# First keys prepared in two halves with their inputs split alike, one block's values copied inside the first chunk, and score tiles taken in another order

## The reference

```python
q, k, v = qkv[:, :, 0], qkv[:, :, 1], qkv[:, :, 2]      # [B, 1024, 16, 8]
q, k = _rmsnorm(q, q_scale), _rmsnorm(k, k_scale)
q, k = _apply_rope(q, k)
logits = jnp.einsum('bqhd,bkhd->bhqk', q * HEAD_DIM ** (-0.5), k)
out = jnp.einsum('bhqk,bkhd->bqhd', jax.nn.softmax(logits, axis=-1), v)
x = _layernorm(x + out.reshape(B, N, C) @ w_proj + b_proj)
h = jax.nn.silu(_tlin(x, w1_w, w1_s)) * _tlin(x, w2_w, w2_s)
h = jax.nn.gelu(_tlin(h, h1_w, h1_s), approximate=False)
h = jax.nn.gelu(_tlin(h, h2_w, h2_s), approximate=False)
x = _layernorm(x + _tlin(h, w3_w, w3_s))
```

## Time and profile before

| what | us |
|---|---|
| median of 3 runs | 377.18 |
| lowest and highest | 376.13, 378.87 |
| the profiled execution, its own time | 374.42 |
| its span, first to last instruction | 372.8 |
| mean granted TensorE clock in it | 0.983 |

### The profile page before, as it was taken

One profiled execution on the slowest core, in us unless ns is written; L12 is line 12 of the kernel. 1 busy time (PEld: TensorE's weight loads), 2 busy tenths in 40 slices (PEclk: granted clock), 3 DMA queues, 4 the chain that ended last, 5 costly groups with the idle time before them and its releaser, 6 DMA issues.

```text
span 372.8 us, 6252 instructions
## 1 busy us (share of the span) xinstructions
PE 339.6 (91%) x2087; PEld 134.4 (36%) x2091; DVE 221.6 (59%) x465; ACT 304.8 (82%) x350; POOL 28.7 (8%) x41
## 2 busy tenths in 40 slices
PE   7889989998999989998999999989999899999980
PEld 2412223222332444442222544433223535335850
DVE  2997978874557624464466462645477163567754
ACT  2699989999999889789999897979998987863330
POOL 2032111102100000001100000011000000011001
PEclk9989999998999999999999999999999999999996
DMA  7829454326212110201110200202021100000001
GB/s 228 288 77 357 134 184 177 150 98 230 85 38 81 48 55 2 69 33 62 67 62 38 89 11 6 94 0 104 24 94 39 68 0 0 0 29 0 2 0 33
DMA packets 12295, 29.42 MB, mean 79 GB/s; under 512 B 1138, under 2 KB 4082, under 8 KB 12274
## 3 DMA queue, kind: packets, MB, share of 16 engines
q1 hardware_dynamic: 8368, 16.23, 12.9%
q0 software_dynamic: 3328, 12.06, 9.0%
q10 hardware_dynamic: 578, 0.85, 0.7%
HBM read 17.64 MB, written 9.44 MB: 73 GB/s over the span
## 4 chain that ended last, share of the span: by engine, by line
PE 65%; DVE 13%; ACT 7%; DMA 6%; issue 5%; POOL 1%; SPq 0%; POOLq 0%; DVEq 0%; ACTq 0%
PE ps L490 24%; PE ps L537 15%; PE ps L476 12%; ACT probs L825 6%; PE ps L527 4%; PE ps L645 4%; DMA va<-v_all 4%; DVE ffn L1042 2%; PE ps L445 2%; PE ps L607 1%; DMA xT<-in_x_t 1%; DMA k_scr<-parts 1%; DVE r L923 1%; PE ps L679 1%; PE ps L507 1%
## 5 line engine op out<-in xcount | busy, mean ns | idle before, releaser
L825 ACT ACTIVATE probs<-ps 128x1024 f32<-128x1024 f32 x256 | 242.9, 1035 | 26.4 <-PE ps L476 26.3
L490 PE MATMUL ps<-probs,va 128*9 128x512 f32 x896 | 113.5, 598 | 2.7 <-ACT probs L825 2.4
L476 PE MATMUL ps<-qa,ka 32*128 32x512 f32 x512 | 76.2, 500 | 9.9 <-ACT probs L825 7.5
L476 PEld LDWEIGHTS ps<-qa,ka 32*128 32x128 f32 x512 | 31.1, 183 | 108.1 <-ACT probs L825 61.6
L1042 DVE TENSOR_SCALAR ffn<-ps,col 128x512 f32<-128x512 f32 x36 | 27.0, 750 | 54.9 <-PE ps L537 50.8
L537 PE MATMUL ps<-g_hi,w_hi 128*128 128x512 f32 x108 | 45.4, 421 | 2.5 <-DVE ffn L1042 2.5
L537 PE MATMUL ps<-g_lo,w_hi 128*128 128x512 f32 x108 | 42.3, 392 | 0.0
L490 PEld LDWEIGHTS ps<-probs,va 128*9 128x9 f32 x896 | 15.8, 89 | 48.1 <-issue 27.7
L537 PEld LDWEIGHTS ps<-g_hi,w_hi 128*128 128x128 f32 x108 | 20.2, 187 | 15.3 <-DVE ffn L1042 4.3
L1017 DVE TENSOR_TENSOR g_lo<-ffn,g_hi 128x512 fp32r<-128x512 f32 x36 | 24.9, 692 | 1.2
L423 POOL TENSOR_TENSOR rs<-ve,mhalf 128x4 f32<-128x4 f32 x6 | 6.1, 1022 | 229.9 <-DVE ve L1005 229.9
(11 more groups left out here) (129 smaller groups left out, 320.7 us busy)
## 6 DMA issues: line engine op xcount, KB each, us to landing
ka<-k_scr SPq DMA_DIRECT2D x14, 512.0 KB
k_scr<-parts POOLq DMA_DIRECT2D x8, 512.0 KB, 4.2
q_scr<-parts POOLq DMA_DIRECT2D x8, 512.0 KB, 5.0
qa<-q_scr SPq DMA_DIRECT2D x14, 256.0 KB
va<-v_all SPq DMA_DIRECT2D x14, 144.0 KB
ffn<-in_h POOLq DMA_DIRECT2D x1, 1024.0 KB, 6.8
h_raw<-in_h POOLq DMA_DIRECT2D x1, 1024.0 KB, 8.7
xT<-in_x_t SPq DMA_DIRECT2D x3, 256.0 KB, 6.6
```

The lines of the kernel that those rows point to most:

```text
L476: mm = pe.matmul(s_tile(u)[:, i, :], ka[rows, slot, kt * P:(kt + 1) * P], qa[rows, slot, :], start=True, stop=not shifted)
L490: mm = pe.matmul(ps[32 * h:32 * h + VW, O_BANK, :], v, probs[:, step % 4, h, :], start=(kt == 0), stop=(kt == KT - 1))
L825: nc.scalar.activation(probs[:, step % 4, 2 * pair:2 * pair + 2, :], s_tile(u), ACT.Exp).then_inc(exp_done, 1)
```

## The change

The change has four parts.

Input DMAs: the weights are stored in the order K, KS, Q, QS, V (`W_AT`) and come in two transfers of 128 KB; x of block 0 comes in two halves of 256 tokens (`HC` = 256 columns), the first on its own semaphore; cosines and sines are one DRAM tensor, loaded by one DMA for tokens 0 to 255, one for 256 to 511 and one for 512 to 1023, all from SyncE. `cols` goes over to ScalarE's queue.

First keys in two halves: projection, square, variance, Ln, Exp, rotation, sum and product of k0 are done for tokens 0 to 255 first, up to the strip rows; the same for tokens 256 to 511 stand behind the queries and the projections of k1. VectorE's order changes with it: the three strips of group 1 come right behind those of group 0, and the parts for the stores of k0 and q0 (`rows_parts(0, ...)`, `rows_parts(1, ...)`) behind them, ahead of those of k1.

Values of block 1: their projection is the new first task of the first chunk (slot 5) and ScalarE copies it behind pair 7. TensorE waits for the copy before the values of key tile 4. Before the first logits it waits for one copy and four logarithms.

Score tiles: they are taken in turn, but at pairs 43 and 54 the second oldest is taken instead of the oldest (`tiles_in_turn`), so that the last three pairs of a chunk have the tiles 0, 1, 2. A pair's logits wait for the exponential that last read its tile.

```diff
-MIX_FIRST = 18
+MIX_FIRST = 19
-TASKS = (("proj", 0), ("swap", 0), ("var", 0),
+W_AT = {K: 0, KS: P, Q: 2 * P, QS: 3 * P, V: 4 * P}
+TASKS = (("v", 1), ("proj", 0), ("swap", 0), ("var", 0),
...
-TASK_SLOTS = (10, 18, 22, 23, 26, 30, 31, 34, 38, 40, 42, 46, 48, 50, 54, 56, 59, 62)
+TASK_SLOTS = (5, 10, 18, 22, 23, 26, 30, 31, 34, 38, 40, 42, 46, 48, 50, 54, 56, 59, 62)
+V_PAIR = 7
+def tiles_in_turn(swaps):
+    order, found = [0, 1, 2], []
+    for u in range(2 * STEPS):
+        if u in swaps:
+            order[0], order[1] = order[1], order[0]
+        found.append(order.pop(0))
+        order.append(found[-1])
+    assert found[-3:] == [0, 1, 2]
+    return found
+TILE_SWAPS = (43, 54)
+TILE_OF = tiles_in_turn(TILE_SWAPS)
...
-            return ps[:, 2 * (u % 3):2 * (u % 3) + 2, :]
+            return ps[:, 2 * TILE_OF[u]:2 * TILE_OF[u] + 2, :]
...
-            sp.dma_start(wq[:, 0:4 * P], w_qkv[:, 0:4 * P]).then_inc(in_w, 16)
-            sp.dma_start(col[:, 0:NCOL], cols).then_inc(in_cols, 16)
-            sp.dma_start(sinT[:, 0:CH], sines[:, 0:CH]).then_inc(in_rope[0], 16)
+            sp.dma_start(wq[:, 0:2 * P], w_qkv[:, 0:2 * P]).then_inc(in_wk, 16)
+            load_tables(0, 0, HC)
+            sp.dma_start(wq[:, 2 * P:4 * P], w_qkv[:, 2 * P:4 * P]).then_inc(in_wq, 16)
+            load_tables(1, HC, CH)
             load_x(1)
             sp.dma_start(wq[:, 4 * P:5 * P], w_qkv[:, 4 * P:5 * P]).then_inc(in_wv, 16)
-            sp.dma_start(sinT[:, CH:SEQ], sines[:, CH:SEQ]).then_inc(in_rope[1], 16)
+            load_tables(2, CH, SEQ)
...
-                wait(pe, exp_done, 64 * c + (u - 2 if u >= 3 else (0, -2, -1)[u]) if u >= 3 or not isinstance(c, int) else 0)
+                before = max(v for v in range(-2 * STEPS, u) if TILE_OF[v % (2 * STEPS)] == TILE_OF[u])
+                if before >= 0 or not isinstance(c, int):
+                    pe.wait_ge(exp_done, 64 * c + before + 1)
...
                 if n == 0:
-                    pe.wait_ge(rot_done, 6)
+                    pe.wait_ge(rot_done, 8)
...
+                    if step == 1:
+                        pe.wait_ge(rot_done, 7)
                     logits(0, step, 0, shifted)
...
+                    if step == KT // 2 + 1:
+                        pe.wait_ge(v_evac, 2)
                     if step:
                         values(0, step - 1)
...
-            pe.wait_ge(in_w, 16)
-            pe.wait_ge(in_x[0], 16)
-            proj(K, ps[:, 0, :], 0).then_inc(qk_proj, 1)
-            proj(KS, ps[:, 1, :], 0).then_inc(qk_proj, 1)
+            pe.wait_ge(in_wk, 16)
+            pe.wait_ge(in_x_first, 16)
+            proj_half(K, ps[:, 0, 0:HC], 0).then_inc(qk_proj, 1)
+            proj_half(KS, ps[:, 1, 0:HC], 0).then_inc(qk_proj, 1)
             pe.wait_ge(in_means, 16)
             pe.wait_ge(sq_done, 1)
-            variance(ps[:, 4, :], sq_k).then_inc(var_ready, 1)
+            variance(ps[:, 5, 0:HC], sq_k[:, 0:HC]).then_inc(var_ready, 1)
+            pe.wait_ge(in_wq, 16)
+            pe.wait_ge(in_x[0], 16)
             proj(Q, ps[:, 2, :], 0).then_inc(qk_proj, 1)
             proj(QS, ps[:, 3, :], 0).then_inc(qk_proj, 1)
...
             proj(K, ps[:, MIX_BANK, :], 1).then_inc(qk_proj, 1)
+            proj_half(K, ps[:, 4, 0:HC], 1).then_inc(qk_proj, 1)
+            pe.wait_ge(ln_done, 1)
+            proj_half(KS, ps[:, 5, 0:HC], 1).then_inc(qk_proj, 1)
             proj(KS, ps[:, O_BANK, :], 1).then_inc(qk_proj, 1)
...
+            project_v(ps[:, 1, :], 0).then_inc(v_proj, 1)
             pe.wait_ge(ln_done, 2)
-            project_v(ps[:, 5, :], 0).then_inc(v_proj, 1)
             pe.wait_ge(sq_done, 3)
-            variance(ps[:, 4, :], sq_k1).then_inc(var_ready, 1)
-            pe.wait_ge(rot_done, 2)
-            project_v(ps[:, 0, :], 1).then_inc(v_proj, 1)
+            variance(ps[:, 0, :], sq_k1).then_inc(var_ready, 1)
+            pe.wait_ge(v_evac, 1)
+            pe.wait_ge(sq_done, 4)
+            variance(ps[:, 1, 0:HC], sq_k[:, HC:CH]).then_inc(var_ready, 1)
...
-            pe.wait_ge(v_evac, 2)
-            pe.wait_ge(ln_done, 3)
+            pe.wait_ge(ln_done, 4)
...
-            act.dma_start(xT[:, 0:CH], x_t[:, 0:CH]).then_inc(in_x[0], 16)
-            act.dma_start(cosT[:, 0:CH], cosines[:, 0:CH]).then_inc(in_rope[0], 16)
+            act.dma_start(xT[:, 0:HC], x_t[:, 0:HC]).then_inc(in_x_first, 16)
+            act.dma_start(col[:, 0:NCOL], cols).then_inc(in_cols, 16)
             act.dma_start(mean8[:], means).then_inc(in_means, 16)
+            act.dma_start(xT[:, HC:CH], x_t[:, HC:CH]).then_inc(in_x[0], 16)
...
+            def late_v(n):
+                act.wait_ge(mix_ready, n + 1)
+                copy_v(1, ps[:, MIX_BANK, :])
+                act.wait_ge(v_evac, 2)
+                act.nop().then_inc(mix_free, 1)
...
+                if u == V_PAIR:
+                    late_v(TASKS.index(("v", 1)))
...
+            turned_half(ps[:, 5, first], KS, 1, rot_k[:, second]).then_inc(rot_done, 1)
+            dve.wait_ge(sq_done, 4)
+            turned_half(ps[:, 4, first], K, 1, h_k[:, second]).then_inc(rot_done, 1)
+            rope_of(7, h_k[:, second], rot_k[:, second], rinv_k[:, second], 3)
+            direct_rows(h_k, HC, HC, 0, C_KLOW, ka[:, 0, second])
             turned_by(ps[:, MIX_BANK, :], K, 1, h_k1).then_inc(rot_done, 1)
-            rope_of(6, h_k1, rot_k1, rinv_k1, 3)
+            rope_of(8, h_k1, rot_k1, rinv_k1, 4)
             direct_rows(h_k1, 0, CH, 0, C_KLOW, ka[:, 0, CH:SEQ])
-            rows_parts(0, 0, 0, h_k)
-            rows_parts(1, 0, 1, h_q)
             direct_rows(h_k, 0, CH, 1, C_KLOW, ka[:, 1, 0:CH])
             direct_rows(h_q, 0, CH, 1, C_QLOW, qa[:, 1])
             direct_rows(h_k1, 0, CH, 1, C_KLOW, ka[:, 1, CH:SEQ])
+            rows_parts(0, 0, 0, h_k)
+            rows_parts(1, 0, 1, h_q)
             rows_parts(2, 1, 0, h_k1)
```

More of the change, by code:

```diff
@@ L98, in wait, with build @@
     eng.wait_ge(sem, count)
-def build(nc, x_t, x_n, w_qkv, cols, scale_rows, bias, w_proj, w1, w2, h1, h2, w3, cosines, sines, means, eye, out):
+def build(nc, x_t, x_n, w_qkv, cols, scale_rows, bias, w_proj, w1, w2, h1, h2, w3, tables, means, eye, out):
     ctx = ExitStack()
@@ L171, in build @@
         prep = probs[:].rearrange("p a h q -> p (a h q)")
-        sq_k, rinv_k, rot_k, sq_q, rinv_q, rot_q, sq_k1 = (prep[:, i * CH:(i + 1) * CH] for i in range(7))
+        sq_k, sq_q, rinv_q, rot_q, sq_k1 = (prep[:, i * CH:(i + 1) * CH] for i in range(5))
         held = [ffn[:, STAGE + i * CH:STAGE + (i + 1) * CH] for i in range(8)]
-        h_k, h_q, h_k1, rinv_k1, rot_k1 = held[0:5]
+        h_k, h_q, h_k1, rinv_k1, rot_k1, rinv_k, rot_k = held[0:7]
         late_sets = (held[5:8], held[2:5])
@@ L444, in proj, with proj_half @@
             def proj(i, bank, t):
-                return pe.matmul(bank, wq[:, i * P:(i + 1) * P], xT[:, t * CH:(t + 1) * CH], start=True, stop=True)
+                return pe.matmul(bank, wq[:, W_AT[i]:W_AT[i] + P], xT[:, t * CH:(t + 1) * CH], start=True, stop=True)
+            def proj_half(i, bank, hf):
+                return pe.matmul(bank, wq[:, W_AT[i]:W_AT[i] + P], xT[:, hf * HC:(hf + 1) * HC], start=True, stop=True)
             def project_v(bank, t):
                 for i in range(TILES):
-                    mm = pe.matmul(bank[:, i * P:(i + 1) * P], xT[:, t * CH + i * P:t * CH + (i + 1) * P], wq[:, V * P:(V + 1) * P],
+                    mm = pe.matmul(bank[:, i * P:(i + 1) * P], xT[:, t * CH + i * P:t * CH + (i + 1) * P], wq[:, W_AT[V]:W_AT[V] + P],
                                    start=True, stop=True)
@@ L776, in square, with logarithm, inverse_root, copy_v @@
                 nc.scalar.activation(dst, bank, ACT.Square).then_inc(sq_done, 1)
-            def inverse_root(n, bank, dst):
+            def logarithm(n, bank, dst):
                 act.wait_ge(var_ready, n)
                 nc.scalar.activation(dst, bank, ACT.Ln, bias=eps_c[:]).then_inc(ln_done, 1)
-                act.wait_ge(ln_done, n)
+            def inverse_root(ln, dst):
+                act.wait_ge(ln_done, ln)
                 nc.scalar.activation(dst, dst, ACT.Exp, scale=-0.5).then_inc(rinv_done, 1)
[L784 to L787, removed]
+            def copy_v(t, bank):
                 for i in range(TILES):
-                    ins = nc.scalar.copy(v_all[:, 0, :, (n - 1) * TILES + i, :, 0:HD],
+                    ins = nc.scalar.copy(v_all[:, 0, :, t * TILES + i, :, 0:HD],
                                          bank[:, i * P:(i + 1) * P].rearrange("p (g h d) -> p g h d", g=NG, h=HG))
@@ L793, in _ @@
             act.wait_ge(qk_proj, 1)
-            square(ps[:, 0, :], sq_k)
-            inverse_root(1, ps[:, 4, :], rinv_k)
+            square(ps[:, 0, 0:HC], sq_k[:, 0:HC])
+            logarithm(1, ps[:, 5, 0:HC], rinv_k[:, 0:HC])
+            inverse_root(1, rinv_k[:, 0:HC])
             act.wait_ge(qk_proj, 3)
             square(ps[:, 2, :], sq_q)
```

(32 more changed lines are left out.)

32 lines of the change are left out of this document (18 added, 14 removed).

## The result

The changed kernel takes 381.62 us (median of 20 runs, 380.40 to 384.25) where the kernel before took 377.01 (20 runs, 373.75 to 381.69) beside it. The ratio is 1.0159 with a 95% interval of 1.0134 to 1.0183: slower by 1.6%, beyond the 1% that I could tell from no change. The profiled execution took 381.76 us, span 380.0. Of the experiments, e10 and e12 have profiles of executions 4 and 6 us above their own medians; from those two only single stretches are read, no totals.

A forecast was written before the change was run, and what follows sets the result against it. It took step 16's wait for the load of group 2 as the first chunk's bound, TensorE behind it. 3.2 + 1.2 + 0.9 - 1.8 = +3.5 us on the median 377.18 gave 380.7 us; own range 379.0 to 382.5, all cases 376.0 to 384.3.

The forecast's parts named there:

- The sum of +3.5 us: Whole kernel: later load +3.2, slow clock +1.2, pair 43 +0.9, chunk boundaries -1.8 us.
- The key parts, moved behind the strips: Stores ahead of step 16: k0 issued at 30.2, k1 landing at 43.7, 5.5 us later issue, bounds 42.5 to 44.7.
- the old stream's thin place: DMA stream from k0's issue to k1's landing: a thinner place before k1's issue would go, saving 0.3 us.
- The opening: Kernel start: TensorE at 5.0, VectorE at 6.9, first logits near 16.2, first exponential near 17.1, 1.2 us earlier.
- The 0.6 us that I had left at pair 8: Opening: some 0.6 us gain left after the values' projection and copy, which only lengthens step 16's wait.
- The load: Load of group 2 for step 16: takes 13.2 us, lands at 57.0 in place of 53.8, +3.2 us.
- rival B: Step 16: load stretched to 15.1 us by weights and q1's store, two slow stretches; +6.7 us, 383.9; chance 0.15.
- The clock behind the wait: TensorE behind step 16's wait: throttled clock costs +1.2 us, bounds 0 and 3.4.
- Score tiles: Three chunk boundaries gain 0.6 us each, -1.8; pair 43 in the first chunk costs +0.9.
- Rival A: Step 16: load lands within 1 us of before and the clock holds; 376.3 us; chance 0.12.
- C: Step 16: the late load without a loss of clock; +2.3 us, 379.5; chance 0.17.
- D: Opening's gain of 0.6 to 1.2 us reaches the end, step 16 not bound by the load; 375.4; chance 0.06.

The follow-up runs named there:

- e10: The changed kernel with h2's load right behind h1 and the weights w1, w2, w3 issued behind q1's store; 373.65 us, ratio 0.9933.
- e12: e1 with the values' task of block 1 in slot 7 in place of 5, no dummy matmuls; 373.25 us, ratio 0.9916.
- e2: The kernel before with only the parts of k0 and q0 moved behind group 1's strips; 383.46 us, ratio 1.0206.
- e4: The changed kernel with 24 dummy matmuls before TensorE waits for the load of group 2; 381.54 us, ratio 1.0128.
- e1: The changed kernel with the parts of k0 and q0 put back ahead of group 1's strips; 373.87 us, ratio 0.9937.
- e3: The kernel before with the new order of score tiles alone; 377.24 us, ratio 1.0000.
- e6: e1 with three dummy matmuls ahead of the first logits; 373.31 us, ratio 0.9916.
- e7: e1 with the first chunk's tile swaps at pairs 45 and 53 in place of 43 and 54; 373.16 us, ratio 0.9922.
- e5: The changed kernel with h2's 1 MB load moved from between the stores to right behind h1; 379.97 us, ratio 1.0088.
- e9: e8 with the weight loads of w1, w2, w3 moved behind q1's store; 373.38 us, ratio 0.9941.
- e11: The kernel before with the weight loads of w1, w2, w3 moved behind q1's store; 375.56 us, ratio 0.9990.
- e8: e1 with h2's load behind h1, three opening dummy matmuls, first-chunk swaps at 45 and 53, values' task in slot 7; 371.36 us, ratio 0.9872.

## Why the prediction was right or wrong

The direction of the mechanism was right, the time of 380.7 us was 0.9 us short of the measured median, and the measured one lay in the range. That it came so near is in part luck. The sum of +3.5 us was read from the profiled execution of 374.42 us; from profile to profile the change cost 7.2 us, twice as much. I added the sum to the median of 377.18, which is 2.8 us above that execution, and the changed kernel has no such distance (381.76 profiled, 381.62 in the median). The two errors nearly cancel. The forecast's words "+0.9%" were too mild: I gave "within 1%" 0.55 and slower by more 0.40, and it was slower by 1.6%.

*The key parts, moved behind the strips: right in its chain, too small in its size.* The step gave 43.8 for SyncE's issue and +3.2 us at step 16; it was 46.41, and +6.7 by TensorE's start, beyond my bound of 6.1. The 3.5 us by which the wait ended later than forecast (60.5 in place of 57.0) are three terms. k0's issue at 30.66 in place of 30.2: 0.5. The stream from there to k1's landing: 15.6 us where I took the old 13.8 less 0.3, so 2.1. The load: 14.1 us where I took 13.2, so 0.9.

The stream's error is a step of its own: I assumed that the old stream's thin place came from the late issue of k1 and would go when k1 was issued early. It grew instead: 1.9 us at 246 GB/s before (31.1 to 33.0), 4.0 us at 246 GB/s in the changed kernel (from 36.6), with 347 and 323 on both sides. From the kernel before:

```profile
31.10:33.00 1.90, 1.48 (x16) 0.49 (x12) 1.80 (x5) 1.90 (x3) 0.01 (x1) 1.00 0.97 246
```

This repeats: from k0's issue to k1's landing the stream takes 15.6 to 15.8 us in the changed kernel, e2 and e4, where k1 is issued 3.5 us behind k0, and 13.8 or 13.9 us in the kernel before, e1, e3, e6, e7 and e12, where it is issued 8.3 us behind. Taking h2 out (e5) took 5.1 us off k1's landing, and the three stores alone ran at 326 GB/s, 3 MB in 9.3 us. That this slow place is h2's load between the stores fits both, but what slows it was not tried.

*The opening.* TensorE started at 4.46 where I took 5.0, and VectorE at 7.65 where I took 6.9. What it waited for was none of the things that I named: the row of scales, now last of five transfers on ScalarE's queue, landed at 6.87 and the flags from it took until 7.65. The first logits at 16.40 and the first exponential at 16.98 are within 0.2 us of my step. The 0.6 us that I had left at pair 8 were wrong in sign: it started at 28.42 where it had been 26.69, with 6.8 us of slow clock and the values' task in step 2 both in it. So TensorE was free for step 16 at 54.51 and not at 51.8, and its wait was 6.03 us long only because the load came so late. As I said, none of this reached the end, since step 16 waited anyway. But e1, where it doesn't wait, is ready for step 16 at 54.31, and the kernel before was ready at 52.79: the new opening starts its logits 1.4 us earlier and arrives 1.5 us later.

*The load.* The rival B's condition did not come: the weights were issued at 43.95, ahead of k1's landing, and all but about 0.1 MB of them (worked out from the GB/s behind 47.8) were through before the load's bytes moved. But its sum of +6.7 is nearer to the 7.2 between the profiles than mine, and what it stood on was right and strong: e5 came to exactly that case and its load took 18.1 us, more than B's 15.1.

*The clock behind the wait: +1.2 forecast, 1.8 measured* (38.07 us from pair 32 on in the changed kernel, 36.27 in e1). Its lower level lasted 6.8 us, 5.1 of them behind the wait. The Trainium skill (TensorE: Matmul & The Clock Gate, HAM oscillation) is borne out: the burst behind the wait of 6.03 us for the DMA started throttled.

*Score tiles: -1.8 and +0.9 forecast, -1.5 and +0.86 measured.* The size is near, its three equal shares are not. The later chunks took 237.80 us against 240.03, -2.2 us, but 0.7 of that is no work of the tiles. The kernel before had a slow stretch at its first boundary which the changed kernel has not. Where both sides have it (e3 against the kernel before) the new order saves 1.5 us, and where neither has (the changed kernel against e2's 239.34) 1.5 us as well. It comes from two boundaries and not from three: ScalarE's idle times of 0.69 and 0.68 us (until 171.88 and 251.81 before) are gone, but at the first boundary it loads a function table (ACT_TABLE_LOAD) for 1.28 us with either order, and TensorE still waits for an exponential there (1.18 us, 1.20 before). e7, with the new order, has the slow stretch again and took 0.6 us more in that chunk. The kernel before, then e7:

```profile
90.40:93.80 3.40, 3.29 (x20) 0.65 (x23) 0.79 (x2) 2.64 (x4) 0.00 (x0) 0.50 0.17 64
...
91.00:94.40 3.40, 3.29 (x18) 0.55 (x20) 1.32 (x4) 2.92 (x4) 0.00 (x0) 0.50 0.10 36
```

With the measured sizes the sum is 7.0 + 1.8 + 0.9 - 2.2 = +7.5, against 7.2 in the spans. Rival A fell with the wait of 6.03 us, C with the clock of 0.50, and D with e1, which frees step 16 and arrives there later than the kernel before was ready.

## What to carry to other kernels

Follow each result of an engine to whoever loads it from DRAM later: VectorE work that looks like mere bookkeeping (casting parts for a store) can be the head of a chain of queue, DMA, queue and DMA that is 30 us long (29.92 to 60.54 here), and moving it behind "more urgent" work moved the end of that chain by 6.7 us for 6.0 at its head. When a transfer on such a chain is made earlier, look at what it now runs beside: taking 1 MB out of the way of one DMA gained 5.1 us at its landing and 1.1 at the consumer, until the weights beside the next one were moved as well. And a wait taken away at a loop's boundary is paid where the buffers' order is changed; a place in front of a wait for the same event cost nothing (e7).

## What the runs showed of the hardware

A load of 0.9 MB in rows from the DRAM scratch moves at only 91 to 94 GB/s with nothing beside it (e9, e10, e11), takes 11.5 to 12.6 us, and stretches to between 15.1 and 18.1 us with 0.75 MB of weights and a 1 MB store beside it, although the DMA engines together were then at 55% (e5, 41.3 to 59.4: 154 GB/s). The time between the load's issue and that of the weights goes with it: weights 2.5 to 4.4 us ahead of the load, 14.0 to 14.7 us (the changed kernel, e2, e4); 3.4 to 4.4 us behind it, 15.1 to 16.2 (the kernel before, e3, e6, e7, e8); 2.9 and 1.4 us behind it, 17.7 and 18.1 (e12, e5). Here, what it ran beside counted for more than how busy the engines were on the whole.

The clock did not follow from the length of one wait. Behind waits at step 16 of 0.66 us (e6, e7) and 1.02 us (before) it stayed at 1.00; behind 1.54 us (e8), 2.19 us (e3) and more it fell to about 0.5. But at the first chunk boundary, where TensorE waits 1.16 to 1.27 us in all fourteen profiles, it fell in five (before 1.20, e3 1.26, e7 1.17, e11 1.27, e12 1.20) and stayed up in nine (e2 with 1.25 and e6 with 1.25 among them).

The kernel before has an opening of two kinds. In its own profile and in e2's the first two projections (four matmuls) take 1.96 us; in e3's and e11's, whose opening is the same, they take 3.75 and 3.57, and the first logits start 1.8 and 1.2 us later than 17.84. From e3:

```profile
5.83 3.75 PE L461 MATMUL ps<-xT,wq 128*128 128x512 f32 x4 [0.90 <-DMA xT<-in_x_t]
```

The granted clock is 1.00 in that stretch in all four, so what slows these matmuls stays open. The ten profiles with the new opening start their logits between 15.9 and 16.6. So the change's opening is steadier as well as earlier, and against the late kind its logits gain 2.7 to 3.3 us and not the 1.4 us that the two profiles show. In e3 the late opening moves the whole chain: k0's store is issued at 26.52 in place of 24.69, and the load lands at 56.77 in place of 53.77. I take this to be why the medians differ by less than the profiles; the times alone don't prove it.
